# Packing ahead of the v loads, an early load of u, and a new order among the first transposes

## The chip, the cores and the metric
The kernel runs on one core of one Trainium2 chip. The metric is the device time of one execution in microseconds. The time before is the median of three runs.

## What is computed
The input is x, 16 images of 64 x 64 positions with 128 channels. One layer follows the other; the last two add their result to their input.

```python
x = x + _L0_conv_ref(_gn(x), ...)      # group norm, then a two-dimensional LSTM over rows and columns
t = _to_tokens(x)                      # (16, 4096, 128)
t = t + _L1_attn_ref(_ln_t(t), ...)    # Nystrom attention, 8 heads, 64 landmarks, + convolution of v
t = t + _L1_ffn_ref(_ln_t(t), ...)     # recurrence over the 4096 tokens
...
# in _L1_attn_ref
out = attn1 @ attn2_inv @ (attn3 @ v)
res = conv(v, conv_w)                  # 33 taps along the tokens
out = (out + res) @ w_out + b_out
return x + out
# in _L1_ffn_ref
Wx = einsum('bti,hi->bth', x, W)
Wx = (Wx - mean) * rsqrt(var + eps) * gamma + beta     # mean and var over all 65536 tokens
y = sigmoid(Wx[:, t] + y @ V.T)        # 4096 steps in turn
```

## The kernel before
Six stages follow each other: group norm, LSTM, landmarks, the inverse of attn2, output, recurrence. The change touches the last two. Engines run programs of their own and meet at semaphores. All DMAs named here are issued by SP in program order, and an SP that waits issues nothing.

**The output stage** (`output_phase`) works through 16 images `b` of 8 chunks `c` of 512 tokens, 128 slots in all. Every engine has a function `slot(b, c, ...)` with a fixed order written out by hand, and `nth(b, c)` is the running number of the chunk from 1. For a chunk:
- TensorE makes the scores (L2175), ScalarE exponentiates (`p1`, L2318), TensorE weighs with the inner matrix and a column of ones (L2185), which gives values and denominators in one. ScalarE copies them to `even` and `odd` (L2310, L2312, semaphore `denc`).
- `pack(b, c)` (L1987): SP copies the denominators of `even` and `odd` with two small DMAs to `den_packed`, 128 x 32. VectorE takes reciprocals into `rec_packed` (L2386, semaphore `rec`).
- `spread(b, c)` (L1996): SP stores `rec_packed` to the scratch row `recips` in HBM, two small DMAs. It waits for `rec` of that chunk, and at L1994 for the previous broadcast to have landed, since that one reads `recips`.
- `broadcast(b, c)` (L2003): SP loads `recips` back, each head's row repeated over 16 partitions, into `rden` (256 KB). It waits for `spread` to have landed.
- VectorE multiplies (`normalise`, L2397), adds the convolved v (L2380, `oT`), TensorE projects (L2211), VectorE adds the base and takes the moments of each token (L2366 to L2372), GpSimd scales (`norm`, L2089, tile `u`), SP stores to `scaled` (L1978), TensorE adds `u`'s products to the statistics of the recurrence (`moments`, L2224).
- In the same slot TensorE convolves a quarter of half an image's v for the next image (L2197). It needs all four pieces of that half; `load_v` (L1553) loads one piece a slot with two DMAs, 544 KB together. The last image has no v loads and no convolution.

VectorE's slot runs: maxima of chunk c + 1, `residual(c - 3)`, `merge(c - 1)`, `reciprocals(c - 1)`, `normalise(c - 2)`, `add_convolved(c - 2)`. SP's slot runs: store, base load, `spread(c - 1)`, v load, `broadcast(c - 1)`, `pack(c)`, load of the tokens. Behind the last slot come the last spread and broadcast and four stores.

**The recurrence** (`recurrence_phase`) works on blocks of 128 tokens of all images. `load_u` (L2507) loads a block of `scaled` into one of five buffers `ub`, four DMAs of 256 KB; four blocks are asked for at the start. Before the first step TensorE makes the sums of the statistics (L2630), waits for the weights (48 on `f_weights`, three DMAs issued by ScalarE's queue at L2784), transposes block 0 (`turn_first`, L2640, four groups; ScalarE copies each to `zT`, L2789), and makes the statistics' products (`spread` at L2763, and two pair products at L2766 and L2768) from which VectorE and GpSimd make scale and shift. Then come the weigh products (L2666), the normalisation, and `lay` (L2678), on which the first step stands. The fourth transposes reuse the first's bank and wait for its copy.

Of the kernel before, what the change touches and what calls it, by code (L numbers as in the profile page):

```python
# [11 lines left out]
P = 128  # L12
B = 16
G = 64
C = 128
# [16 lines left out]
class Memory:  # L32


    def __init__(self, nc, ctx):
        self.nc, self.ctx = nc, ctx
# [271 lines left out]
NG = NT // GT  # L308
# [40 lines left out]
class Kept:  # L349
# [4 lines left out]
    def __init__(self, m, sems):  # L354
        self.fwc = m.sb("k_fwc", [C, C])
        self.rstd = m.sb("k_rstd", [P, B, NT])
        self.sums = m.sb("k_sums", [P, MOMENTS])
        self.weight = m.sb("k_weight", [P, 1 + C])
        self.ready = sems.sem("k_ready")

    def fill_weight(self, pool):

# [1515 lines left out]
def output_phase(nc, sems, R, E, K, xnt, tokens, vals, recips, scaled):  # L1878


    with ExitStack() as ctx:
        m = Memory(nc, ctx)
# [43 lines left out]
        s_ust = [sems.sem(f"o_ust{k}") for k in range(2)]  # L1926
        SETUP = 4

        def nth(b, c):

            return NG * b + c + 1

        def wait(eng, name, count):

            if count > 0:
                eng.wait_ge(s[name], count)
# [27 lines left out]
        @block.sync  # L1964
        def _(sp):
            def load_tokens(b, c):
                E.load_tokens(sp, xnt, b, c)

            def load_base(b, c):
                E.load_base(sp, tokens, b, c)  # L1970

            def load_v(b, half, piece):
                E.load_v(sp, vals, b, half, piece)

            def store_scaled(b, c):
                wait(sp, "u", nth(b, c))
                b0, c0 = at(b, c)
                sp.dma_start(scaled[b0, 512 * c0:512 * c0 + 512, :].rearrange("(n p) c -> p n c", p=P), u[c % 2][:, :, 1:1 + C]  # L1978
                             ).then_inc(s_ust[c % 2], 16)

            def pack(b, c):

                wait(sp, "denc", 2 * nth(b, c))
                wait(sp, "rec", nth(b, c) - 1)
                for h, tile in enumerate((even[c % 2], odd[c % 2])):
                    row = DH * (1 - h)
                    sp.dma_start(den_packed[LM * h:LM * h + LM, :], tile[row:C:QUAD, :].rearrange("g (j e) -> g j e", j=DH)  # L1987
                                 ).then_inc(s_packed, 16)

            def spread(b, c):  # L1990

                wait(sp, "rec", nth(b, c))
                if nth(b, c) > 1:
                    sp.wait_ge(s_rden, 16 * (nth(b, c) - 1))  # L1994
                for h in range(2):
                    sp.dma_start(recips.rearrange("(g a) (j e) -> a g j e", a=2, j=DH)[h], rec_packed[LM * h:LM * h + LM, :]  # L1996
                                 ).then_inc(s_spread, 16)

            def broadcast(b, c):

                sp.wait_ge(s_spread, 32 * nth(b, c))
                wait(sp, "att", nth(b, c) - 2)
                sp.dma_start(rden[c % 2][:, :], recips.unsqueeze(1).broadcast_to([HEADS, DH, 512])).then_inc(s_rden, 16)  # L2003

            def slot(b, c, q, first, last):
                if precedes(c, 4, first):
                    store_scaled(b, c - 4)
                if precedes(c, 3, first) and follows(c, 1, last):
                    wait(sp, "res", nth(b, c - 3))
                    load_base(*at(b, c + 1))  # L2010
                if precedes(c, 1, first):
                    spread(b, c - 1)

                if c < GT and b + 1 < B:
                    wait(sp, "conv", NG * (b + 1))
                    load_v(b + 1, 1, c)
                if c >= GT and b + 2 < B:
                    wait(sp, "conv", NG * (b + 1) + GT)
                    load_v(b + 2, 0, c - GT)
                if precedes(c, 1, first):  # L2020
                    broadcast(b, c - 1)
                pack(b, c)
                if follows(c, 6, last):

                    wait(sp, "qm", nth(b, c + 2))
                    load_tokens(*at(b, c + 6))
            wait(sp, "conv", GT)
            for piece in range(GT):
                load_v(1, 0, piece)
            for c in range(4, 6):  # L2030
                wait(sp, "qm", c - 3)
                load_tokens(0, c)

            each_image(sp, slot)
            spread(B - 1, NG - 1)
            broadcast(B - 1, NG - 1)
            for c in range(NG - 4, NG):
                store_scaled(B - 1, c)
            for q in range(2):
                sp.wait_ge(s_ust[q], 16 * B * NG // 2)  # L2040
# [395 lines left out]
def recurrence_phase(nc, sems, K, scaled, ffn_v_t, gamma, beta, out):  # L2436
# [4 lines left out]
    with ExitStack() as ctx:  # L2441
        m = Memory(nc, ctx)
        UB = 5
# [15 lines left out]
        moved = m.sb("f_moved", [C, 1])  # L2459
        shift = m.sb("f_shift", [C, 1])  # L2460
        std = m.sb("f_std", [P, B, NT])
        ub = [m.sb(f"f_u{k}", [P, B, C]) for k in range(UB)]
        zT = [m.sb(f"f_zT{q}", [C, RT, B]) for q in range(2)]
        wxn = [m.sb(f"f_wxn{q}", [C, RT, B]) for q in range(2)]
        y = [m.sb(f"f_y{q}", [C, RT, B]) for q in range(2)]
# [3 lines left out]
        turned = [m.ps(f"f_turned{k}", [P, 4, C]) for k in range(2)]  # L2469
        zt = m.ps("f_zt", [C, 4, P])  # L2470
# [7 lines left out]
        s_setup = sems.sem("f_setup")  # L2478
        s_stat = sems.sem("f_stat")
        s_bn = sems.sem("f_bn")  # L2480
        s_u = [sems.sem(f"f_u{k}") for k in range(UB)]
        s_zt = sems.sem("f_zt")
        s_zc = sems.sem("f_zc")
        s_wx = sems.sem("f_wx")
# [17 lines left out]
        def _(sp):  # L2502
# [12 lines left out]
            def body(T, q, first, last):  # L2515
                for g in range(GR):
                    if not first:
                        store(T - 1, 1 - q, g)
                    if T + UB - 1 < BLOCKS:
                        load_u(T + UB - 1, g)  # L2520
            for X in range(UB - 1):
                for g in range(GR):
                    load_u(X, g)
            each_block(body)
# [99 lines left out]
        def _(pe):  # L2624
# [10 lines left out]
            def turn_first(g, bank):  # L2635

                if g == 0:
                    pe.wait_ge(s_u[0], 16 * GR)
                for j in range(4):
                    mt = nc.tensor.transpose(bank[:, j, :], ub[0][:, 4 * g + j, :], ident[:, :])  # L2640
                mt.then_inc(s_zt, 1)
# [115 lines left out]
                    if spare:  # L2757
                        keep_warm()

            for g, bank in enumerate((zt, turned[0], turned[1])):  # L2760
                turn_first(g, bank)
            pe.wait_ge(s_bn, 1)
            nc.tensor.matmul(spread, full[:, 1:1 + C], K.fwc[:, :], start=True, stop=True, skip_group_check=True).then_inc(s_stat, 1)  # L2763
            pe.wait_ge(s_zc, 1)
            turn_first(3, zt)
            nc.tensor.matmul(pair[:, 0:1], K.fwc[:, :], full[:, 0:1], start=True, stop=True, skip_group_check=True)  # L2766
            pe.wait_ge(s_bn, 2)
            nc.tensor.matmul(pair[:, 1:2], prod[:, :], one[:, :], start=True, stop=True, skip_group_check=True).then_inc(s_stat, 1)  # L2768
            for k, bank in enumerate((wxp[0], wxp[1], turned[0], turned[1])):
                at_bank = bank if k < 2 else bank[:, :, :].rearrange("c j t -> c (j t)").rearrange("c (t b) -> c t b", b=B)  # L2770
                for piece in range(PIECES):
                    weigh(0, 0, k, piece, at_bank)
# [85 lines left out]
```

## Time and profile before

| | us |
|---|---|
| median of 3 runs (5888.39 to 5891.15) | 5889.22 |
| the profiled execution | 5894.68 |
| its span, first to last instruction | 5892.9 |
| TensorE busy in the span | 5223.6 (89%) |
| VectorE busy | 3058.7 (52%) |
| ScalarE busy | 3136.4 (53%) |
| GpSimd busy | 1516.7 (26%) |
| span up to the output stage | 2514 |
| output stage | 1063 |
| recurrence | 2315 |

The profile is one execution. PE is TensorE's matmul, PEld its weight load, DVE VectorE, ACT ScalarE, POOL GpSimd, and SPq what SP issues. L with a number is a line of the kernel. Times on a row are microseconds from the start of the span. A share of busy time says little of what a stage waits for; that is read from the waits of the stage, where an engine's idle time is put down to the instruction or DMA that ended it.

### The profile page before, as it was taken

How to read it: one execution, taken by the hardware profiler on the slowest of the kernel's cores; microseconds unless marked ns; L12 is line 12 of the kernel's file. 1: busy time of each engine (PE TensorE's matmuls, PEld its weight loads, DVE VectorE, ACT ScalarE, POOL GpSimd, SP SyncE). 2: the span in 40 equal slices, each digit the busy share in tenths (PEclk: the TensorE clock that was granted, in tenths of full speed). 3: DMA queues.
4: the chain of work that ended last, by engine and by line, in shares of the span. 5: the costliest groups of instructions: out<-in, count | busy, mean ns of one | idle time of the engine just before them, and what ended most of it. 6: DMA issues, size and time to landing. Idle time of an engine off the chain costs nothing. (4 is left out here: it accounts for less than half of the span.)

```text
span 5892.9 us, 223296 instructions
## 1 busy us (share of the span) xinstructions
PE 5223.6 (89%) x97395; PEld 3271.2 (56%) x97488; DVE 3058.7 (52%) x8152; ACT 3136.4 (53%) x9108; POOL 1516.7 (26%) x1905
## 2 busy tenths in 40 slices
PE   5599999997899888799999997888888888888888
PEld 4599888896566666645555443333333333333333
DVE  8677777775888886568888882111111111111111
ACT  6455555564677776478888883333333333333333
POOL 2100000001888875246666661000000000000000
PEclk7899999999999999999999998999999999999999
DMA  9631111225887773457777762111111111111100
GB/s 389 272 116 58 58 58 58 73 77 183 253 246 236 238 243 116 103 162 207 207 208 207 204 175 66 32 32 32 34 33 32 32 33 34 32 32 32 35 18 24
DMA packets 773031, 689.32 MB, mean 117 GB/s; under 512 B 67056, under 2 KB 663024, under 8 KB 767984
## 3 DMA queue, kind: packets, MB, share of 16 engines
q1 hardware_dynamic: 754672, 575.39, 32.8%
q0 software_dynamic: 14672, 95.16, 4.0%
q8 instruction: 743, 12.17, 0.9%
q10 hardware_dynamic: 2736, 4.89, 0.2%
q14 instruction: 208, 1.70, 0.1%
HBM read 392.17 MB, written 274.89 MB: 113 GB/s over the span
## 5 line engine op out<-in xcount | busy, mean ns | idle before, releaser
L2796 ACT ACTIVATE f_y<-f_acc 128x16 f32<-128x16 f32 x4096 | 753.8, 184 | 1541.3 <-PE f_acc L2738 1541.3
L2738 PEld LDWEIGHTS f_acc<-f_y,f_vT 128*32 128x32 f32 x32768 | 644.8, 108 | 1436.7 <-ACT f_y L2796 1436.1
L2738 PE MATMUL f_acc<-f_y,f_vT 128*32 128x16 f32 x32768 | 1045.7, 193 | 278.1 <-issue 0.4
L2696 PE MATMUL f_junk<-f_idle 128*32 128x512 bf16 x8400 | 831.9, 376 | 0.0
L2578 DVE COPY f_zT<-f_zt 128x512 f32<-128x512 f32 x124 | 85.8, 692 | 1136.6 <-PE f_zt L2652 1136.6
L2355 DVE TENSOR_REDUCE o_m<-o_bank_l 128x8 bf16<-128x512 f32 x512 | 328.8, 683 | 98.7 <-PE o_bank_l L2152 98.7
L2571 DVE TENSOR_SCALAR f_wxn<-f_wxp,f_scale,f_shift 128x512 f32<-128x512 f32 x126 | 102.0, 810 | 508.8 <-PE f_wxp L2666 508.8
L1299 ACT ACTIVATE a_p<-a_s 128x512 f32<-128x512 f32 x502 | 259.2, 602 | 153.6 <-PE a_s L1166 151.7
L533 POOL DMA_DIRECT2D hidden<-l_h x46 | 34.6, 754 | 1162.8 <-DVE l_hsum L790 961.5
L712 ACT ACTIVATE l_gate<-l_pf,r_ctx 128x256 f32<-128x256 f32 (+7 forms) x512 | 202.4, 446 | 229.8 <-PE l_pf L643 229.6
L2318 ACT ACTIVATE o_p<-o_bank_s 128x512 f32<-128x512 f32 x512 | 264.4, 602 | 101.2 <-PE o_bank_s L2175 101.2
L2591 DVE SCALAR_TENSOR_TENSOR f_sum<-f_u,f_std,f_turned 128x128 f32<-128x128 f32 x512 | 143.4, 342 | 317.9 <-PE f_turned L2689 317.9
L2696 PEld LDWEIGHTS f_junk<-f_idle 128*32 128x32 bf16 x8400 | 249.9, 99 | 0.0
L1359 DVE TENSOR_REDUCE a_m3p<-a_s 128x1 f32<-128x512 f32 x360 | 223.4, 682 | 50.0 <-PE a_s L1126 48.5
L633 PE MATMUL l_pio<-l_x,r_k_lm 128*128 128x256 f32 (+7 forms) x1024 | 239.0, 356 | 0.2 <-ACT l_gate L729 0.2
L633 PE MATMUL l_pf<-l_x,r_k_lm 128*128 128x256 f32 (+7 forms) x1024 | 238.9, 356 | 0.0
L647 PE MATMUL l_pio<-l_hsum,r_ctx 128*128 128x256 f32 (+7 forms) x1024 | 238.8, 356 | 0.0
L2302 ACT ACTIVATE o_base<-o_base,r_loss,r_gain 128x128 f32<-128x128 f32 x512 | 225.4, 497 | 0.0
L2689 PE MATMUL f_turned<-f_ident,f_y 128*32 128x128 f32 x4096 | 221.3, 290 | 0.5 <-DVE f_sum L2591 0.5
L1017 POOL TENSOR_TENSOR a_r<-a_vare,a_half 128x8 f32<-128x8 f32 x128 | 209.7, 1639 | 10.0
L712 ACT ACTIVATE l_gate<-l_pio,r_ctx 128x256 f32<-128x256 f32 (+7 forms) x512 | 203.3, 450 | 14.0
L2678 PE MATMUL f_acc<-f_wxn,f_ident 128*32 128x128 f32 x4096 | 207.1, 274 | 0.8 <-issue 0.8
(323 smaller groups left out, 11466.4 us busy)
## 6 DMA issues: line engine op xcount, KB each, us to landing
o_v<-vals SPq DMA_DIRECT2D x256, 272.0 KB
a_hid<-hidden SPq DMA_DIRECT2D x112, 520.0 KB, 5.0
hidden<-l_h POOLq DMA_DIRECT2D x46, 1040.0 KB, 6.8
l_x<-skew SPq DMA_DIRECT2D x46, 1024.0 KB, 5.2
vals<-a_v SPq DMA_DIRECT2D x128, 272.0 KB, 3.6
gn_x<-in_x SPq DMA_DIRECT2D x16, 2048.0 KB, 18.0
a_xin<-in_x SPq DMA_DIRECT2D x128, 256.0 KB, 4.9
tokens<-a_t SPq DMA_DIRECT2D x128, 256.0 KB, 3.4
```

The costliest lines, as they stand in the source:

```text
L633: mm = nc.tensor.matmul(banks[c][g][:, :, rows], w[W[g]], xs, start=g in (0, 2, 3), stop=False, skip_group_check=True)
L647: mm = nc.tensor.matmul(banks[c][g][:, :, rows], w[U[g]], hsum[:, lanes[c], rows], start=False, stop=True, skip_group_check=True)
L712: nc.scalar.activation(gate[:, g, lanes[c], rows], banks[c][g][:, :, rows], ACT.Tanh if g == 2 else ACT.Sigmoid, bias=bias[BI[g]]).then_in ...
L1299: nc.scalar.activation(p3[c % 2][g][:, :], score_bank(i, c, g), ACT.Exp).then_inc(s["exp"], 1)
L1359: nc.vector.tensor_reduce(m3p[:, g, c:c + 1], bank[:, :], AX.X, ALU.max).then_inc(s["mx"], 1)
L2302: nc.scalar.activation(bs[c % 4][:, k, :], bs[c % 4][:, k, :], ACT.Identity, scale=R.gain[:, b, n:n + 1], bias=R.loss[:, b, n:n + 1]).then ...
L2318: nc.scalar.activation(p1[g][:, :], bank_s[g][:, :], ACT.Exp).then_inc(s["exp"], 1)
L2355: nc.vector.tensor_reduce(m1[:, 2 * r:2 * r + 2, LM * half:LM * half + LM].rearrange("p k (g r) -> p k g r", r=QUAD)[:, :, :, 0:2], bank_l ...
L2689: mt = nc.tensor.matmul(turned[g % 2][rows, b % 4, :], y[q][:, rows, b], ident[:, :], start=True, stop=True)
L2696: nc.tensor.matmul(junk[rows, :], idle[:, 0:QUAD], idle[:, :], start=True, stop=True)
L2738: mm = nc.tensor.matmul(acc[k % 2][rows, t, :], vT[:, rows], before, start=False, stop=True, skip_group_check=True)
L2796: nc.scalar.activation(y[q][:, step, :], acc[step // RC % 2][:, step % RC, :], ACT.Sigmoid).then_inc(s_y, 1)
```

## The change
Three things.
- In SP's slot `pack(b, c)` stands behind `spread(b, c - 1)` and ahead of the v loads and `broadcast(b, c - 1)`, instead of behind that broadcast.
- Block 0 of u gets a buffer and a semaphore that outlive the output stage (`K.head`, `K.s_head`). SP loads it behind the last broadcast and ahead of the last four stores, once the stores of chunk 2 of the last image have landed; the recurrence no longer loads it.
- Before the first step, TensorE's order is: transposes 0, product `spread`, transposes 1, the pair products, transposes 2, transposes 3. It was: transposes 0, 1, 2, `spread`, transposes 3, the pair products.

```diff
@@ class Kept
+        self.head = m.sb("k_head", [P, B, C])
+        self.s_head = sems.sem("k_head")
@@ output_phase, SP's slot
                 if precedes(c, 1, first):
                     spread(b, c - 1)
-
+                pack(b, c)
                 if c < GT and b + 1 < B:
                     wait(sp, "conv", NG * (b + 1))
                     load_v(b + 1, 1, c)
...
                 if precedes(c, 1, first):
                     broadcast(b, c - 1)
-                pack(b, c)
@@ output_phase, SP behind the slots
             spread(B - 1, NG - 1)
             broadcast(B - 1, NG - 1)
+            sp.wait_ge(s_ust[0], 8 * nth(B - 1, NG - 5))
+            for g in range(B // 4):
+                sp.dma_start(K.head[:, 4 * g:4 * g + 4, :], scaled[4 * g:4 * g + 4, 0:P, :].rearrange("b p c -> p b c")
+                             ).then_inc(K.s_head, 16)
@@ recurrence_phase
-        ub = [m.sb(f"f_u{k}", [P, B, C]) for k in range(UB)]
+        ub = [K.head] + [m.sb(f"f_u{k}", [P, B, C]) for k in range(1, UB)]
-        s_u = [sems.sem(f"f_u{k}") for k in range(UB)]
+        s_u = [K.s_head] + [sems.sem(f"f_u{k}") for k in range(1, UB)]
-            for X in range(UB - 1):
+            for X in range(1, UB - 1):
@@ recurrence_phase, TensorE before the first step
-            for g, bank in enumerate((zt, turned[0], turned[1])):
-                turn_first(g, bank)
+            turn_first(0, zt)
             pe.wait_ge(s_bn, 1)
             nc.tensor.matmul(spread, full[:, 1:1 + C], K.fwc[:, :], ...)
-            pe.wait_ge(s_zc, 1)
-            turn_first(3, zt)
+            turn_first(1, turned[0])
             nc.tensor.matmul(pair[:, 0:1], K.fwc[:, :], full[:, 0:1], ...)
             pe.wait_ge(s_bn, 2)
             nc.tensor.matmul(pair[:, 1:2], prod[:, :], one[:, :], ...).then_inc(s_stat, 1)
+            turn_first(2, turned[1])
+            pe.wait_ge(s_zc, 1)
+            turn_first(3, zt)
```

## Rows read from the trace of the kernel before

**Rows 1.** Busy time of the engines in the output stage, clock, DMA share and rate.
```profile
2514.00:3577.00 1063.00, 994.00 (x12042) 518.73 (x12040) 853.45 (x2179) 866.39 (x1794) 693.25 (x705) 0.98 0.69 193
```

**Rows 2.** Order of time, SP: first and last `spread` of 111 slots.
```profile
2579.59 0.55 SPq L1996 DMA_DIRECT2D recips<-o_rec_packed  x1
...
3469.85 1.15 SPq L1996 DMA_DIRECT2D recips<-o_rec_packed  x2
```

**Rows 3.** Waits, 2579 to 3470: who for whom: us in total, times, longest.
```profile
DVE o_rec_packed L2386 <- DMA o_den_packed<-o_odd: 56.7, 80, 1.8
...
PE o_bank_x L2211 <- DVE o_oT L2380: 23.6, 28, 2.4
...
PE o_bank_s L2197 <- DMA o_v<-vals: 6.8, 8, 1.3
```

**Rows 4.** SP's own waits in the same stretch.
```profile
SPq L1994 <- DMA o_rden<-recips: 101.5, 94, 2.1
SPq L1996 <- DVE o_rec_packed L2386: 69.6, 100, 1.8
SPq L2003 <- DMA recips<-o_rec_packed: 11.0, 22, 1.4
```

**Rows 5.** Order of time, SP, one slot: start, duration, what.
```profile
3011.47 1.14 SPq L1996 DMA_DIRECT2D recips<-o_rec_packed  x2
3012.66 1.01 SPq L1553 DMA_DIRECT2D o_v<-vals  x2
3013.85 0.63 SPq L2003 DMA_DIRECT2D o_rden<-recips  x1
3014.58 0.56 SPq L1987 DMA_DIRECT2D o_den_packed<-o_even  x1
...
3017.68 0.51 SPq L1547 DMA_DIRECT2D o_base<-tokens  x1
3019.56 1.15 SPq L1996 DMA_DIRECT2D recips<-o_rec_packed  x2
```

**Rows 6.** SP's waits between the last two of these.
```profile
SPq L1994 <- DMA o_rden<-recips: 0.6, 1, 0.6
```

**Rows 7.** Order of time, ScalarE and TensorE in that slot.
```profile
3008.56 0.59 ACT L2312 ACTIVATE o_odd<-o_bank_s 128x512 f32<-128x512 f32 x1
...
3018.12 1.11 PE L2197 MATMUL o_bank_s<-o_v,o_bands 128*64 128x256 f32 x8
```

**Rows 8.** Order of time, SP and TensorE: a late v load.
```profile
3076.80 1.01 SPq L1553 DMA_DIRECT2D o_v<-vals  x2
...
3082.82 1.11 PE L2197 MATMUL o_bank_s<-o_v,o_bands 128*64 128x256 f32 x8 [1.33 <-DMA o_v<-vals]
```

**Rows 9.** Order of time, SP: first and last `spread` of nine slots, last image.
```profile
3492.47 1.15 SPq L1996 DMA_DIRECT2D recips<-o_rec_packed  x2
...
3559.67 1.15 SPq L1996 DMA_DIRECT2D recips<-o_rec_packed  x2
```

**Rows 10.** SP's waits, 3494 to 3545, seven slots of the last image.
```profile
SPq L2003 <- DMA recips<-o_rec_packed: 10.2, 7, 2.3
SPq L1996 <- DVE o_rec_packed L2386: 6.4, 7, 1.2
```

**Rows 11.** Order of time, end of the output stage and opening of the recurrence.
```profile
3567.04 1.07 POOL L2089 TENSOR_TENSOR o_u<-o_t,k_rstd 128x512 f32<-128x512 f32 x1 [0.18 <-DMA scaled<-o_u]
...
3573.76 1.04 POOL L2089 TENSOR_TENSOR o_u<-o_t,k_rstd 128x512 f32<-128x512 f32 x1
...
3578.44 0.45 ACTq L2784 DMA_DIRECT2D f_beta<-in_L_ffn_beta  x1
...
3584.55 1.09 PE L2640 MATMUL f_zt<-f_ident,f_u 128*128 128x128 f32 x4 [5.08 <-DMA f_u<-scaled]
...
3589.28 1.95 PE L2666 MATMUL f_wxp<-f_zT,k_fwc 128*32 128x128 f32 x64 [0.35 <-ACT f_zT L2789]
```

**Rows 12.** DMA issues, 3560 to 3600: count, KB each, us to landing.
```profile
f_beta<-in_L_ffn_beta ACTq DMA_DIRECT2D x1, 0.5 KB, 3.8
```

## The prediction

> **What bounds the kernel now.** I read the busy time by stages first [rows 1]. The output stage takes 1063 us of 5892.9; the recurrence behind it, 4096 steps of TensorE and ScalarE in turn, is untouched but for its opening. So the change is decided in the output stage: 128 slots (16 images of 8 chunks), each with the same program on every engine.
>
> A slot lasts 8.02 us on the mean. Its mark here is S, the moment at which SP issues `spread`; 111 slots lie between S = 2579.59 and S = 3469.85 [rows 2]. The engines' waits in that stretch [rows 3] say what TensorE lacks: its projection (L2211) waited for VectorE's o_oT 28 times, 23.6 us, its convolution (L2197) for the v loads 8 times, 6.8 us. (23.6 + 6.8) / 111 = 0.27, so an undisturbed slot takes 7.75 us. VectorE in turn waited for the packed denominators (L2386) 80 times, 56.7 us. That row is what the change aims at; read alone it promises 0.27 us a slot.
>
> SP's own waits [rows 4] say more. Before `spread(c)` SP waits first for the previous broadcast to have landed (L1994: 94 times, 101.5 us), then for the reciprocal (L1996: 100 times, 69.6 us). The reciprocal is last, but the broadcast landed only 69.6 / 111 = 0.63 us earlier, and in 11 slots nothing but the broadcast was waited for. Two loops run through SP, one 0.6 us ahead of the other:
> - denominators: S, v loads, broadcast, pack, landing, reciprocal, next S;
> - broadcast: S, v loads, broadcast, landing, next S (the scratch row recips must be free again).
>
> One slot in full [rows 5]: S at 3011.47, v issued 3012.66, broadcast 3013.85 (S + 2.38), the first pack 3014.58, base over at 3018.19. There SP waits 0.6 us for the broadcast [rows 6], which thus landed at 3018.8, 7.3 us after S and 4.9 after its issue; 0.7 us later the reciprocal is there, and S is 3019.56. Read so, 94 slots have a landing (this one stands for them): median 7.19 us behind S and 5.99 behind v's first issue, mean 7.37 behind S; 80% lie within 5.7 to 6.8 behind v's issue.
>
> **The change part by part.**
>
> *pack(c) ahead of the v loads and the broadcast.* It is two DMA issues of 0.56 [rows 5] with gaps of 0.05, 1.21 us. Its own waits cost nothing: the o_even and o_odd that it needs were done at 3009.15 [rows 7], 3.5 us before the place (3012.66) to which it moves, and the reciprocal before it is what `spread` has just waited for. Behind it stand v and the broadcast, both 1.21 us later; tokens, store and base keep their time, since the sum of issues ahead of them is the same.
> Gained: pack's second issue goes from S + 3.7 to S + 1.8, so the reciprocal is last no more, and VectorE's 56.7 us of waiting go. Late next is the broadcast. Nothing in the rows makes its landing shorter: grouped by the time since base was issued (2 to 3.5 us before v), the medians behind v's issue are 5.9, 6.0 and 6.4 us, so the queue in front of v is as good as empty already, and v's bytes stay 1.2 us ahead of the broadcast as now.
> New slot by the median: 1.19 + 1.21 + 5.99 + 0.05 = 8.44 us. By the mean: 7.37 + 1.21 + 0.05 = 8.63, less 11.0 / 111 = 0.10 for the 22 broadcasts that waited for `spread` to land (L2003, [rows 4]) and no more would: 8.53. I take 8.45, nearest to the median, which fits most slots: +0.43, times 111 = **+48 us**. Bounds: the whole of the mean, 8.63: +68; a shift of only 0.7 us, if issues and landings that now block take up the rest: 8.05, +3. The bound below nothing is the third rival.
>
> A rule of the Trainium skill gives another result. "DMA: Bandwidth & Descriptors", section "Anatomy of one DMA — SWDGE (gpsimd) path", has about 2.0 us plus bytes / 436 GB/s for a DMA. An estimate by that page: v and broadcast (800 KB) would land 3.9 us behind v's issue, the broadcast's loop would be 6.3 us, and TensorE would bound the slot. By that rule, the trace disagrees: 5.99 us where it has 3.9.
>
> *v loads 1.2 us later.* The convolution of chunks 0 and 4 needs the half whose last piece was loaded in the slot before. In the worst case seen, v issued 3076.80, the convolution ran at 3082.82 after 1.33 us of waiting [rows 8]: landed 6.0 us behind its issue. Undisturbed, the convolution stands at S + 6.65 (3018.12, [rows 7]). With v at S + 2.4 and landings of 4.6 to 6.0 it is 0.3 to 1.7 us too late in 28 slots. In a slot of 8.45 TensorE has 0.7 us to spare, which hides most: cost 0, up to +5. Without that cover it is 28 x 0.3 to 1, 8 to 28 us.
>
> *Last image.* It has no v loads; a slot takes (3559.67 - 3492.47) / 9 = 7.47 us [rows 9]. There the broadcast is held by the landing of `spread` (L2003, 10.2 us in 7 slots, [rows 10]); pack fills just this gap and delays nothing, and the 6.4 / 7 = 0.9 us by which the reciprocal comes last go. I take 0.5 of them, as VectorE's own work is close behind: 9 x 0.5 = **-4 us** (0 to -8).
>
> *Block 0 of u in the tail.* The semaphore count it waits for is that of a store issued 20 us earlier, so it costs no wait. Four issues of 0.55 stand ahead of the last four stores, and 1 MB in front of them in the queue. Store 4 frees the buffer that L2089 takes at 3567.04 (0.18 us waited, [rows 11]); with 2.2 us of issue and the bytes in front (up to 5.4 us by the stage's mean of 193 GB/s, [rows 1], though here the stage's other loads are over) that becomes 3569 to 3574. The last product of L2089 starts at 3573.76 anyhow, behind VectorE, which covers most of this span: cost 0, up to 2.
> At the opening TensorE waited 5.08 us for u, until 3584.55 [rows 11]. Next in its way is the wait for the weights: f_beta was issued 3578.44 and takes 3.8 us to land [rows 12], 3582.2. Gain 2.3.
>
> *Statistics among the transposes.* The weigh products start at 3589.28 [rows 11], behind the fourth zT copy; the small pair products are hidden in that gap now. Afterwards the product into junk (0.63 us) and they stand ahead of the last transposes, so weigh starts 0.7 later. Scale and shift come 1.2 us earlier, which the first steps don't need, as they are laid behind the weigh products. +0.7. Opening and tail together: **-1.6 us** (-3 to +1).
>
> Sum: 48 - 4 - 1.6 = +42. The profiled execution took 5894.68 us around its span of 5892.9, 5.5 above the median of the runs, 5889.22. It becomes 5937, the median **5931 us**.
>
> **The rivals.**
> 1. *The broadcast's landing is the bound* (forecast, 0.62): slots of 8.27 to 8.6, own range 5911 to 5950.
> 2. *The shift is mostly absorbed* (0.15). SP's v issues, 1.0 us now and up to 1.9 in a fifth of the slots, no more block, and `spread`'s landing hides behind pack. Shift 0.6 to 0.8, slots of 8.0 to 8.1: 5884 to 5905. Against it: the landing doesn't depend on the gap before v.
> 3. *TensorE is the bound* (0.20), the other side. It decides once the broadcast lands within 5.3 us of v's first issue (S + 7.7). Slot 7.75, 111 x 0.27 = 30, of which late v loads take 8: -22 - 4 - 1.6, 5862; at best 5852. For it: the denominators are the wait that ends most slots now, and the skill's rule. Against it: fewer than one landing in ten is below 5.7.
> 4. *v decides on top* (0.03): landings of 6 us in all 28 slots, +28: 5960.
>
> **How the numbers follow.** The range 5856 to 5950 leaves out about 0.08 on either side. 0.2% is 12 us, about what a measurement of this kernel can tell from no change. Slower (above 5901): case 1, case 4 and a fifth of case 2, 0.68; the rest of case 2 is "same", 0.12; faster 0.20.
>
> **What would show it.** Right: the wait of L2386 for o_den_packed is gone; SP waits some 2 us at L1994 in nearly every slot and not at L1996; VectorE's L2397 waits for o_rden often, and TensorE's L2211 for o_oT behind it; S to S is 8.4, broadcast at S + 3.6. Wrong: S to S of 7.7 with little waiting at L2397 (rival 3), or L2197's wait as TensorE's longest (rival 4). The opening: the first transpose 4.7 instead of 7 us behind the stage's start.

## The result, and the profile after

The change made the kernel slower: 6003.4 us (median of 4 runs) beside 5888.8 before on the same chip, ratio 1.0197 [1.0184, 1.0209], +115 us. The profiled executions show 108 of them: spans of 6001.0 and 5892.9 us. Forecast were 5931, and a range of 5856 to 5950. The direction was right, the size was not.

All of it is in the output stage, now 1173 us long (2514 to 3686.8, where GpSimd's first instruction of the next stage starts) where it took 1064 (2514 to 3577.6) [rows 1]. TensorE's granted clock over the stage is 0.96 where it was 0.98, near its 2.4 GHz level in both; its busy time grew by 26 us, a quarter of the difference at most. DMA share and rate fell with the longer slots. The windows view of after, of the output stage and 3 us of the next; the columns are length, busy time and count of PE, PEld, DVE, ACT and POOL, then granted clock, DMA share, GB/s:

```profile
2514.00:3690.00 1176.00, 1020.28 (x12054) 532.70 (x12052) 887.16 (x2182) 869.61 (x1796) 714.93 (x710) 0.96 0.65 176
```

SP's waits after, in a stretch that holds 110 of its slots (line waited at, what ended the wait: us in total, times, longest). They answer to [rows 4]:

```profile
SPq L1996 <- DMA o_rden<-recips: 297.3, 110, 4.3
SPq L1549 <- DVE o_t L2371: 41.3, 55, 2.3
SPq L1998 <- DVE o_rec_packed L2391: 3.9, 9, 0.8
```

L1996 is the old L1994, the wait in front of `spread` for the last broadcast. It went from 94 waits of 1.1 us to 110 of 2.7: SP waits for the broadcast's landing in every slot. L1998, the old L1996, is the reciprocal's wait: from 69.6 us in 100 slots to 3.9 in 9. The denominators' loop is off the path, the broadcast's loop is all of it. The waits for `spread` to land (L2003 before) are gone.

The engines' waits in the same stretch, which answer to [rows 3]:

```profile
DVE o_att L2402 <- DMA o_rden<-recips: 133.1, 99, 2.7
ACT o_even L2315 <- PE o_bank_s L2190: 115.1, 76, 4.9
PE o_bank_x L2216 <- DVE o_oT L2385: 98.2, 75, 2.5
PE o_bank_s L2202 <- DMA o_v<-vals: 16.9, 13, 2.3
```

VectorE no longer waits for the packed denominators, it waits for the broadcast (L2402, the old L2397) in 99 slots. TensorE's projection (L2216, the old L2211) waits behind it: 98 us where it was 24.

One slot of SP's timeline after (start, us, instruction), to be laid beside [rows 5]:

```profile
3030.21 1.14 SPq L1998 DMA_DIRECT2D recips<-o_rec_packed  x2
3031.45 0.58 SPq L1989 DMA_DIRECT2D o_den_packed<-o_even  x1
3032.08 0.55 SPq L1989 DMA_DIRECT2D o_den_packed<-o_odd  x1
3032.67 1.00 SPq L1555 DMA_DIRECT2D o_v<-vals  x2
3033.78 0.62 SPq L2005 DMA_DIRECT2D o_rden<-recips  x1
3034.45 0.45 SPq L1546 DMA_DIRECT2D o_xnT<-xnt  x1
3034.94 0.97 SPq L1980 DMA_DIRECT2D scaled<-o_u  x1
3035.96 0.51 SPq L1549 DMA_DIRECT2D o_base<-tokens  x1
3039.09 1.14 SPq L1998 DMA_DIRECT2D recips<-o_rec_packed  x2
```

The broadcast is issued at S + 3.57, where it was S + 2.38. SP's list is done at 3036.5; it waits there 2.6 us for the broadcast, which lands at 3039.0, 5.3 us behind its issue. Just then VectorE's `normalise` starts, and the reciprocal had been done for 1.7 us. SP's wait in 3036.4:3039.2, and two instructions from VectorE's timeline of the same slot (in brackets the idle time before, and what ended it):

```profile
SPq L1996 <- DMA o_rden<-recips: 2.6, 1, 2.6
```

```profile
3037.04 0.34 DVE L2391 RECIPROCAL o_rec_packed<-o_den_packed 128x32 f32<-128x32 f32 x1
3039.13 0.81 DVE L2402 TENSOR_TENSOR o_att<-o_att,o_rden 128x512 f32<-128x512 f32 x1 [1.74 <-DMA o_rden<-recips]
```

Below, every kernel is read in the same way over the same 111 slots. S is the issue of `spread`, B that of the broadcast; its landing is the end of SP's wait for it, so that it is read only in slots that have such a wait. v's lead is the time from v's first issue to B. Means, worked out from SP's timelines and waits (before, 94 of the 111 slots have such a wait, after all of them):

| kernel | slot, us | B behind S | v's lead | landing behind B | landing behind v's first issue | wait for the landing, us in 111 slots | wait for the reciprocal |
|---|---|---|---|---|---|---|---|
| before | 8.02 | 2.61 | 1.41 | 4.75 | 6.16 | 101 | 68 |
| after | 8.99 | 3.63 | 1.15 | 5.27 | 6.41 | 300 | 4 |

After, the three terms make the slot: 3.63 + 5.27 + 0.10 (landing to S) = 9.00. 111 x (8.99 - 8.02) = 108 us, the whole difference of the spans; the last image gives back 2 us, and the slots outside the 111 and that image take about as much.

### The profile page after: what moved, and what is told of

Read it like the earlier page. It is cut to its first block and busy times, and to the rows that moved or that the text cites. A ratio compares the mean times of both kernels' runs of the same rounds, so it can differ in the third digit from the quotient of the medians.

```text
span 6001.0 us, 223389 instructions
## 1 busy us (share of the span) xinstructions
PE 5259.3 (88%) x97488; PEld 3287.0 (55%) x97488; DVE 3092.5 (52%) x8152; ACT 3133.1 (52%) x9108; POOL 1536.3 (26%) x1905
## 5 line engine op out<-in xcount | busy, mean ns | idle before, releaser
L2216 PE MATMUL o_bank_x<-o_wo,o_oT 128*128 128x128 f32 x1024 | 156.3, 298 | 109.6 <-DVE o_oT L2385 109.2
L2216 PEld LDWEIGHTS o_bank_x<-o_wo,o_oT 128*128 128x128 f32 x1024 | 130.7, 200 | 211.6 <-DVE o_oT L2385 210.1
L2596 DVE SCALAR_TENSOR_TENSOR f_sum<-f_u,f_std,f_turned 128x128 f32<-128x128 f32 x400 | 112.1, 343 | 202.0 <-PE f_turned L2694 202.0
```

The costliest lines, as they stand in the source:

```text
L2216: mt = nc.tensor.matmul(bank_x[:, k, :], oT[:, P * k:P * k + P], wo[:, :], start=True, stop=True)
```

## The experiments

Each edit is shown against the kernel before unless it is said otherwise. "One run" is a single execution; the four each of the kernels before and after lie within 0.15%. There the slot, a mean of 111, is the better measure. Kernels with the same order in SP's slot show how well such a mean repeats: slots of 8.99, 9.06 and 9.07 us and landings of 5.27, 5.31 and 5.26 us behind B (after, e1, e15), landings of 4.75 and 4.72 (before, e2).

### Which of the three edits it is

**e1_pack_alone**: only `pack(b, c)` is moved.

```diff
                     spread(b, c - 1)
-
+                pack(b, c)
                 if c < GT and b + 1 < B:
...
                     broadcast(b, c - 1)
-                pack(b, c)
```

> The kernel before with pack(c) moved ahead of the v loads, nothing else. If the slot order is the whole cause: 5995 to 6005, slots of 9.0 us from S to S, SP waiting for the broadcast before every spread, and the last image faster by 0.2 us a slot. If the early load of u or the new order of the transposes carries part of the loss, this kernel is 10 us or more faster than the changed one.

**e2_rest_alone**: the changed kernel with `pack` put back behind the broadcast; the early load of u and the order of the transposes stay.

```diff
                     spread(b, c - 1)
-                pack(b, c)
+
                 if c < GT and b + 1 < B:
...
                     broadcast(b, c - 1)
+                pack(b, c)
```

> The changed kernel with pack(c) put back behind the broadcast: block 0 of u in the tail and the new order among the transposes alone. By the two traces the opening is 0.6 us shorter (17.08 to 16.50 from the stage's start to the first step) and the tail 0.5 us longer (the GpSimd product waits 5.0 us for a store), so 0 within 2 us. The prediction had -1.6. The rival, that it costs, would show 5 us or more.

Measured: e1 6012.1 beside 5895.9, ratio 1.0196 [1.0179, 1.0213], slot 9.06; e2 5895.3, ratio 0.9999 [0.9990, 1.0009], slot 8.02. The moved `pack` is the whole loss. The other two edits together can't be told from nothing.

### Whether the broadcast's place sets the slot

**e3_v_pack_bc**: `pack` goes ahead of the broadcast, but v stays in front of it. B is as late as after, v as early as before.

```diff
                     load_v(b + 2, 0, c - GT)
+                pack(b, c)
                 if precedes(c, 1, first):
                     broadcast(b, c - 1)
-                pack(b, c)
```

> Order in SP's slot: spread, v loads, pack, broadcast. The broadcast is issued as late as in the changed kernel (S + 3.6), v as early as before (S + 1.2). Theory A, the broadcast lands some 6 us behind the first v issue, because v's bytes are ahead of it, and at the earliest 3.7 us behind its own issue: landing at S + 7.2 to 7.4, TensorE bounds with slots of 7.75, 5855 to 5870. Theory B, it lands 4.7 to 5.3 us behind its own issue whatever is ahead: S + 8.3 to 8.9, slots of 8.4 to 9.0, 5935 to 6000.

Measured: 5907.8, ratio 1.0022 [1.0012, 1.0031], slot 8.12, between the two expectations. B is even later than after (S + 3.80), but it lands 4.20 us behind its issue, not 5.27. One slot of SP's timeline, and its waits in 2579:3470:

```profile
3022.08 1.15 SPq L1996 DMA_DIRECT2D recips<-o_rec_packed  x2
3023.27 1.01 SPq L1553 DMA_DIRECT2D o_v<-vals  x2
3024.38 0.58 SPq L1987 DMA_DIRECT2D o_den_packed<-o_even  x1
3025.01 0.56 SPq L1987 DMA_DIRECT2D o_den_packed<-o_odd  x1
3025.66 0.60 SPq L2003 DMA_DIRECT2D o_rden<-recips  x1
```

```profile
SPq L1994 <- DMA o_rden<-recips: 191.2, 109, 2.6
SPq L1996 <- DVE o_rec_packed L2385: 7.4, 12, 1.8
```

So 1.2 us of delay for B alone cost 0.1 us a slot, while 1.2 us for v and B together cost 0.97. The reciprocal's wait is gone here as well, and the landing stands in its place. B in itself is not what counts: v is issued ahead of the broadcast, and when it is issued on time its transfer is under way while SP issues `pack`. The median landing is 6.0 us behind v's first issue before, 6.4 after and 6.7 here, where v's lead is 2.6 us; the mean behind B is 4.75, 5.27 and 4.20. So a landing goes neither by v's issue nor by B alone.

**e4_v_first**: v ahead of `spread`, so that no bytes of v follow it. The order is v, spread, pack, broadcast.

```diff
-                if precedes(c, 1, first):
-                    spread(b, c - 1)
-
                 if c < GT and b + 1 < B:
...
                 if precedes(c, 1, first):
-                    broadcast(b, c - 1)
+                    spread(b, c - 1)
                 pack(b, c)
+                if precedes(c, 1, first):
+                    broadcast(b, c - 1)
```

> Order: v loads, spread, pack, broadcast. v goes out while SP would wait for the reciprocal; the broadcast is issued at S + 2.5 with v's bytes long ahead. Theory A: it lands 3.7 to 4.2 us behind its issue, S + 6.2 to 6.7, TensorE bounds: slots of 7.7, 5850 to 5865. Theory B: S + 7.2 to 7.8, slots of 7.8 to 7.9, 5865 to 5880.

Measured: 6012.6, ratio 1.0197 [1.0180, 1.0214], slot 9.09: a miss, since neither expectation had `spread` itself held up. The broadcast lands 4.13 us behind B now, but B stands at S + 4.83. SP's waits in 2579:3470, and a slot of its timeline:

```profile
SPq L2003 <- DMA recips<-o_rec_packed: 177.2, 98, 2.7
SPq L1994 <- DMA o_rden<-recips: 47.2, 85, 1.2
```

```profile
3029.83 2.05 SPq L1996 DMA_DIRECT2D recips<-o_rec_packed  x2
3031.99 0.57 SPq L1987 DMA_DIRECT2D o_den_packed<-o_even  x1
3032.59 0.55 SPq L1987 DMA_DIRECT2D o_den_packed<-o_odd  x1
3034.86 0.60 SPq L2003 DMA_DIRECT2D o_rden<-recips  x1
```

Between 3033.1 and 3034.9 SP waits for `spread` to have landed. The two small stores of 8 KB each now have v's 544 KB in front of them, and are in `recips` only 4.8 us behind the first's issue in the mean, 5.0 in this slot. In the last image of the kernel before, which has no v, it was 2.4 us at the least and 2.7 in the mean (B at S + 2.39 and S + 2.68). v's bytes were moved from the front of one DMA to that of another on the same loop.

**e7_bc_v_332**: v behind the broadcast, its eight pieces dealt out as 3, 3, 2 and 0 to four slots. The order is spread, pack, broadcast, v.

```diff
                     spread(b, c - 1)
-
+                pack(b, c)
+                if precedes(c, 1, first):
+                    broadcast(b, c - 1)
+                lot = ((0, 3), (3, 6), (6, 8), (8, 8))[c % GT]
                 if c < GT and b + 1 < B:
                     wait(sp, "conv", NG * (b + 1))
-                    load_v(b + 1, 1, c)
+                    for n in range(*lot):
+                        load_part(b + 1, 1, n)
...
-                if precedes(c, 1, first):
-                    broadcast(b, c - 1)
-                pack(b, c)
```

> Order: spread, pack, broadcast, v loads, and v's eight DMAs of a half spread as 3, 3, 2, 0 over its four slots, so that none is due in the slot behind it. Theory A (a DMA waits for the bytes in front of it): neither spread nor broadcast has v in front; broadcast issued at S + 2.5, landed at S + 6.7, TensorE bounds: slots of 7.7 to 7.8, 30 us less than before in the first 15 images, 4 us less in the last: 0.994 of the time before. Theory B (what delays the broadcast is the number of issues and bytes of the slot, wherever they stand): slots of 8.0 or more, no gain.

Measured: 5989.5 beside 5896.8, ratio 1.0154 [1.0140, 1.0168], slot 8.85: a miss. The broadcast lands 4.22 us behind B, as it should, but v is still on its way when the next `spread` is issued. B is at S + 4.32. SP's waits and one of ScalarE's, in 2579:3470:

```profile
SPq L2009 <- DMA recips<-o_rec_packed: 163.1, 90, 3.3
SPq L2000 <- DMA o_rden<-recips: 68.3, 58, 2.4
```

```profile
ACT o_base L2310 <- DMA o_base<-tokens: 96.7, 64, 4.1
```

L2009 is the wait for `spread` to land, as in e4. The base load, queued behind v as well, comes late for ScalarE.

The changed kernel, e3, e4 and e7 together say what is special about v's old place. `spread` lands 2.4 us behind S at the soonest, and B can't come before. v is issued right behind `spread`, so its 1.0 us of issue and the first part of its transfer fall into this wait. In the other three places its bytes were in front of something on the loop that was needed at once.

**e10_half_v**: the changed order, v loaded for 64 of the 128 partitions only.

```diff
             def load_v(b, half, piece):
-                E.load_v(sp, vals, b, half, piece)
+                for side in range(2):
+                    row = 2048 * half + 512 * piece + LM * side
+                    sp.dma_start(v[half][side][0:LM, GT * piece:GT * piece + GT, :],
+                                 vals[b, row:row + 512, :].rearrange("(n p) c -> p n c", p=P)[0:LM]).then_inc(s_v[half], 16)
```

> The order spread, pack, v, broadcast, and each v load takes 64 of 128 partitions (half of v is left out). Theory A: v's bytes cost the broadcast 1.1 us (5.3 against 4.2 in the last image), so half of them cost some 0.5: landing 4.6 to 4.8 behind its issue, slots of 8.4. If v's bytes are of no account, the landing stays at 5.3.

Measured: one run of 5972.8; slot 8.64, landing 4.65 us behind B, which is at S + 3.92. The landing follows v's bytes: 4.1 to 4.2 us with none just in front (e4, e7, and the last image of after), 4.65 with half, 5.27 with all. Not all of the step to 4.65 is bytes: v's two issues took longer here, and its lead was 1.43 us, not 1.15. Behind v's first issue the landing went from 6.41 to 6.07.

### Why the landing takes 0.5 us longer than before

The landing went from 4.75 to 5.27 us behind B, and that half of the loss was in no case of the forecast. Three things changed around the broadcast. `pack`'s DMAs stand in front of v now. The tokens, the store and the base load follow the broadcast 0.69 us behind B rather than 1.95. And v's lead shrank: its median went from 1.20 to 1.10 us, its mean from 1.41 to 1.15. In the old order SP waited for `spread` between v and the broadcast in 22 slots (11.0 us, [rows 4]), and v's two issues took 1.11 us in the mean; in the new one that wait is gone and they take 1.00. The first two have experiments of their own, the third is read from the same traces below.

**e9_pack_wide**: the changed order, and `pack` copies 64 rows of the weights `wo` instead of the scattered denominators. Two DMAs of the same size in another shape.

```diff
-                    row = DH * (1 - h)
-                    sp.dma_start(den_packed[LM * h:LM * h + LM, :], tile[row:C:QUAD, :].rearrange("g (j e) -> g j e", j=DH)
+                    sp.dma_start(den_packed[LM * h:LM * h + LM, :], wo[0:LM, 0:512 // DH]
```

> The order spread, pack, v, broadcast, and pack copies 64 rows of 128 bytes of a weight instead of 4 partitions' 16 pieces each: same bytes, same issues, same waits, but spread over the partitions. The real denominators are left out. In the changed kernel the broadcast lands 5.3 us behind its issue (4.75 before). If pack's narrow source in front of v and broadcast makes the 0.5, it falls to 4.7 to 4.9 and the slot from 9.0 to 8.5; if it is what follows the broadcast, both stay.

Measured: one run of 6018.7; slot 9.13, landing 5.24. The gather from scattered partitions is not the cause. That two small DMAs stand in front of v at all was not varied by this.

**e8_small_followers**: the changed order; tokens and base are loaded for 16 of 128 partitions. **e14_small_followers_before**: the same in the order before.

```diff
-                E.load_tokens(sp, xnt, b, c)
+                sp.dma_start(xnT[c % 4][0:16, :], xnt[b, 0:16, 512 * c:512 * c + 512]).then_inc(s_xl[c % 4], 16)
...
-                E.load_base(sp, tokens, b, c)
+                sp.dma_start(bs[c % 4][0:16, :, :], tokens[b, 512 * c:512 * c + 512, :].rearrange("(n p) c -> p n c", p=P)[0:16]
+                             ).then_inc(s_bl[c % 4], 16)
```

> The order spread, pack, v, broadcast, and the loads of tokens and base behind it take 16 of 128 partitions (the rest of both is left out). If the traffic that now follows the broadcast by 0.65 us instead of 1.9 makes the 0.5 us, the broadcast lands 4.7 or less behind its issue, slots of 8.5; if it is pack in front, it stays at 5.2 to 5.3 and slots at 8.9 to 9.0.

> The kernel before, with the loads of tokens and base cut to 16 of 128 partitions (the rest is left out). If these loads' bytes hold up v and broadcast, the broadcast lands 4.2 to 4.5 behind its issue instead of 4.75 and the slot falls from 8.02 to 7.8. If only followers closer than 1 us matter, both stay.

Measured: e8 one run of 5953.8, slot 8.53, landing 4.79; e14 one run of 5877.5, slot 7.87, landing 4.50. Without most of those bytes the broadcast lands 0.48 us sooner in the new order and 0.25 in the old, so that 0.23 of the 0.52 are theirs. But 0.29 stay (4.50 to 4.79). The base load also stands ahead of `spread` and so in front of v, where it was cut as well; v's loads landed a median 3.3 us behind their issue in e8 and 3.4 in after, so that this can't be much. e11 and e16 move what follows and cut nothing.

**e11_pack_last**: the old order of v and broadcast, `pack` behind the tokens. The followers come 0.68 us behind B, as after, with nothing moved ahead of v.

```diff
                     broadcast(b, c - 1)
-                pack(b, c)
...
                     load_tokens(*at(b, c + 6))
+                pack(b, c)
```

> The kernel before, pack(c) behind the tokens' load: order spread, v, broadcast, tokens, pack. Nothing new is ahead of the broadcast; only its follower comes at 0.65 us instead of 1.9. If followers hold the broadcast up, it lands later behind its issue than before: 5.0 to 5.3 instead of 4.75. If not, 4.75. The reciprocal comes 0.5 us later either way, so the slot is 8.5 to 8.7.

Measured: one run of 5979.2; slot 8.74, landing 5.09 us behind B. The closer followers add at most 0.34 us: v's lead is 1.24 here, 0.17 shorter than before, and behind v's first issue the landing is 6.32, 0.16 more than before. SP's waits in 2579:3520:

```profile
SPq L1994 <- DMA o_rden<-recips: 161.4, 108, 2.8
SPq L1996 <- DVE o_rec_packed L2385: 126.6, 105, 2.1
```

`pack` is later here, so the reciprocal's wait is up as well (1.2 us a slot). This run tells of the landing, not of a better place.

**e15_spaced_after**: the changed order, with a wait for `pv` of the current chunk ahead of the tokens, to put the followers back. **e16_spaced_by_next**: the same with `pv` of the next chunk.

```diff
                     broadcast(b, c - 1)
-                pack(b, c)
+                wait(sp, "pv", nth(b, c))
                 if follows(c, 6, last):
```

```diff
-                pack(b, c)
                 if follows(c, 6, last):
-
+                    wait(sp, "pv", nth(b, c) + 1)
```

> The order spread, pack, v, broadcast, and SP waits before the tokens' load until TensorE has weighed this chunk (about S + 5.5), so that tokens, store and base follow the broadcast by 1.9 us or more, as in the kernel before, with all their bytes. If the follower's distance makes the longer landing, the broadcast lands 4.75 to 4.85 behind its issue instead of 5.3, slots of 8.5: some 55 us above the time before instead of 115. If the bytes in front do it, the landing stays at 5.2 to 5.3 and the slot at 9.0 or more.

> As the spaced kernel before it, whose wait had long passed when SP came to it (6 waits, 2.3 us in all), now with the weighing of the next chunk, which ends about S + 5.5. Tokens, store and base follow the broadcast by 1.9 us, with all their bytes. If the follower's distance makes the longer landing, it is 4.75 to 4.85 behind the broadcast's issue instead of 5.3 and slots are 8.5. If it stays at 5.2 to 5.3, what is in front does it, or the order as such, and slots are 9.0 or more.

Measured: e15 6020.0 beside 5897.1, ratio 1.0211 [1.0194, 1.0228], slot 9.07. Its wait was over when SP came to it nearly every time (6 waits, 2.3 us in all), the followers stayed at 0.7 us behind B, and it says nothing. In e16 they stand 1.93 us behind B, as before: 5995.6 beside 5897.1, ratio 1.0158 [1.0140, 1.0177], slot 8.81, landing 5.06. SP's waits in 2579:3470:

```profile
SPq L1994 <- DMA o_rden<-recips: 155.9, 88, 4.0
SPq L1544 <- PE o_bank_s L2184: 118.3, 97, 3.4
```

So with v and B late and the followers where they were, 0.25 us of landing (5.31 in e1 to 5.06) and 0.25 of the slot come back. The expectation had all of the 0.5 or nothing. e8 with e14 and e16 put the followers' part at 0.23 and 0.25 us, e11 at 0.34 with a shorter lead of v in it.

The rest behind B is 0.2 to 0.3 us, about what v's lead lost in the mean. Counted from v's first issue it is nearly gone:

| followers | old order | new order |
|---|---|---|
| 1.9 us behind B | 6.16 (before) | 6.21 (e16) |
| 0.7 us behind B | 6.32 (e11) | 6.41 (after) |
| tokens and base cut to an eighth | 5.92 (e14) | 5.94 (e8) |

This doesn't prove the lead to be the cause. Within the kernel before, the 56 slots with a lead under 1.3 us (mean 1.19) land 4.85 behind B and the 18 with one over 1.7 (mean 2.04) land 4.45, so that a longer lead gives back about half of its length; by that, 0.26 us less of it are worth some 0.12. And in slots with a lead under 1.3 alone (mean 1.19 in the old order, 1.11 in the new) the landing is 4.85 before and 5.03 in e16, 4.54 in e14 and 4.81 in e8: 0.2 to 0.3 us are between the two orders there as well. So v's lead is likely part of the rest, and how much is not settled; no run takes `pack`'s two DMAs from in front of v with the rest as it is. The last image, without v, grew by 0.26 (3.91 to 4.17, ten slots), but its landings before scatter from 3.5 to 5.0, so that it tells little.

### A pack that delays nothing

**e12_pack_two_buffers**: `den_packed` twice, with a semaphore each, so that `pack(b, c)` can go ahead of `spread(b, c - 1)`, into SP's idle time. **e13_two_buffers_spaced**: the same, with a wait of SP ahead of the tokens that was to put the followers back.

```diff
-        den_packed = m.sb("o_den_packed", [P, 512 // DH])
+        den_packed = [m.sb(f"o_den_packed{k}", [P, 512 // DH]) for k in range(2)]
...
-                wait(sp, "rec", nth(b, c) - 1)
+                wait(sp, "rec", nth(b, c) - 2)
...
+                pack(b, c)
                 if precedes(c, 1, first):
                     spread(b, c - 1)
-
...
                     broadcast(b, c - 1)
-                pack(b, c)
```

```diff
                     broadcast(b, c - 1)
-                pack(b, c)
+                wait(sp, "scaled", GT * (nth(b, c) - 1) + 2)
                 if follows(c, 6, last):
```

> den_packed has two buffers and pack(c) goes ahead of spread(c - 1), into the time in which SP waits anyway: order pack, spread, v, broadcast, tokens. No wait of pack's own, v and broadcast at S + 1.2 and S + 2.4 as before. The reciprocal is no more last. If the bytes and issues in front of v are the cause of the loss, the slot is bound by the broadcast's landing alone, 7.4 plus up to 0.5 for the follower at 0.65 us, or by TensorE, 7.75: slots of 7.75 to 7.95, 10 to 35 us less than before. If packing early is itself the harm, slower than before.

> As the one with two buffers, and SP waits between broadcast and tokens until ScalarE has scaled the first half of the base (about S + 3.8), so that the follower is as far behind as before. If the follower's distance counts, the broadcast lands 4.7 behind its issue and the slot is 7.75 to 7.85, 5 to 15 us less than with the follower at once. If not, equal within 3 us.

Measured: e12 5885.5, ratio 0.9993 [0.9983, 1.0003], slot 7.97; e13 5886.0, ratio 0.9998 [0.9988, 1.0007], slot 7.90. Neither can be told from the kernel before, and both are 2% faster than the changed one. e13's wait was mostly over when SP came to it (29 waits, 9.6 us in all): its followers stand 0.74 us behind B, those of e12 0.68. So e13 is e12 once more and says nothing of the followers. e12's waits of SP and of two engines in 2579:3470:

```profile
SPq L1547 <- DVE o_t L2365: 71.9, 79, 2.9
SPq L1987 <- ACT o_odd L2311: 60.5, 94, 1.5
SPq L2003 <- DMA recips<-o_rec_packed: 50.1, 61, 2.1
SPq L1994 <- DMA o_rden<-recips: 23.5, 35, 2.1
```

```profile
DVE o_att L2396 <- DMA o_rden<-recips: 38.5, 50, 2.5
PE o_bank_x L2210 <- DVE o_oT L2379: 22.6, 20, 2.4
```

The reciprocal's wait is gone and the landing is waited for in 35 slots, not 94. Yet TensorE's projection waits 22.6 us where it waited 23.6 [rows 3]. SP now waits for the denominators' copies (L1987) and for the landing of `spread`, and B slips to S + 3.0. VectorE waits for nothing packed any more, yet the slot is only 0.05 us shorter in e12 and 0.12 in e13, where [rows 3] alone promised 0.27, and no more than the measurement can tell.

## Why the prediction was right and wrong

**The bound.** Right. Read from [rows 4] it was that the broadcast's loop runs 0.6 us behind the denominators' and takes over at once. After, the landing is waited for in 110 slots, the reciprocal in 9, VectorE no more for `den_packed`, and TensorE for VectorE behind it, as the signs listed. In e12 and e13, where the denominators come early and v keeps its place, the slot stays within 0.12 us of before: of the 57 us in [rows 3] little was to be had that way.

**The shift of B.** Right: the sign named was S + 3.6, by the means 2.61 + 1.21 - 0.10 = 3.72, and it is 3.63. But v moved by more than B, from S + 1.20 to S + 2.48. "v's bytes stay 1.2 us ahead of the broadcast as now" holds for the median (1.20, now 1.10) and not for the mean (1.41, now 1.15). Rival 2's absorption took place here, between v and B, and bought nothing, as the landing didn't come sooner with B.

**The landing.** This step failed: "Nothing in the rows makes its landing shorter", and with that the sum kept 5.99 us behind v's first issue. It measured 6.41, 0.42 more. Of these 0.17 are the median taken for the mean (6.16 in the same 94 slots), and 0.25 are growth, 111 x 0.25 = 28 us. Counted from B the growth is 0.52, 111 x 0.52 = 58 us, as v's lead shrank too. I had looked for what could shorten the landing and never priced what could lengthen it. The grouping that was to show its independence looked at what stands in front of v. What stands behind the broadcast was overlooked, though the change moved it: "tokens, store and base keep their time" was said as a thing that costs nothing, and it means that they come 1.2 us closer to a broadcast that comes later. e16, and e8 with e14, show that this is worth 0.25 and 0.23 us; e11 bounds it at 0.34. Of the remainder behind B, 0.2 to 0.3 us, some 0.1 may be v's shorter lead; the cause of the rest stays open.

**Median or mean.** A small failure: the forecast took the median, "which fits most slots", 8.45 rather than 8.53. A sum over 111 slots is a matter of the mean, and this left out 9 us. The 8.53 itself took off 0.10 for the waits for `spread`, as if a sooner B had brought a sooner landing. The 0.05 from landing to S is 0.10 in the mean. By the terms of the sum: v behind S 2.48 for 2.40, the landing 6.41 for 5.99, landing to S 0.10 for 0.05, together 0.55, beside 8.99 - 8.44.

**The rule of the Trainium skill.** The estimate by "DMA: Bandwidth & Descriptors" put the landing at 3.9 us behind v's first issue. The page states its 2.0 us plus bytes / 436 GB/s for DMAs issued by GpSimd; the forecast put it to DMAs of SP. The trace disagrees again, and by more: 6.4 after. With no bytes of v just in front, the broadcast alone takes 4.1 to 4.2 us (e4, e7). It spoke for rival 3, which fell.

**v loads.** Right: TensorE's convolution waited 16.9 us in 13 slots, 6.8 in 8 before, and the slot is full with the broadcast's loop alone (9.00 of 8.99), so that this costs nothing.

**The last image.** Overrated: 7.47 to 7.23 us a slot (mean of ten), 9 x 0.24 = 2 us, not 4. The reciprocal did not stop being last there. SP's waits after in 3597:3653, beside [rows 10]:

```profile
SPq L1996 <- DMA o_rden<-recips: 8.2, 7, 1.6
SPq L1998 <- DVE o_rec_packed L2391: 4.3, 6, 1.2
```

B is at S + 2.52 there and was at 2.68: as forecast, the two `pack` issues fit into the wait for `spread` where no v fills it, and delay nothing. But the broadcast lands 4.17 us behind B, not 3.91, which takes back what the reciprocal gave.

**Tail and opening.** Right in the sum, near nothing (e2: 0.9999). GpSimd did wait in the tail, for the store queued behind block 0's 1 MB, which VectorE's work no longer covered: from the last `spread` to the next stage it is 18.38 us and was 17.90, inside the forecast's 0 to 2. From GpSimd's timeline after:

```profile
3680.59 1.04 POOL L2094 TENSOR_TENSOR o_u<-o_t,k_rstd 128x512 f32<-128x512 f32 x1 [5.02 <-DMA scaled<-o_u]
3682.95 1.04 POOL L2094 TENSOR_TENSOR o_u<-o_t,k_rstd 128x512 f32<-128x512 f32 x1
```

In the opening the first transpose stands 4.49 us behind the stage's start, forecast 4.7, and it waits for f_beta, as named. The weigh products follow 5.34 us behind it rather than 4.73: +0.6, forecast +0.7. From TensorE's timeline after:

```profile
3691.26 1.11 PE L2645 MATMUL f_zt<-f_ident,k_head 128*128 128x128 f32 x4 [2.58 <-DMA f_beta<-in_L_ffn_beta]
3696.60 1.95 PE L2671 MATMUL f_wxp<-f_zT,k_fwc 128*32 128x128 f32 x64 [0.69 <-ACT f_zT L2795]
3703.02 0.51 PE L2683 MATMUL f_acc<-f_wxn,f_ident 128*32 128x128 f32 x9 [2.07 <-issue]
```

From the stage's start to the first step it is 16.50 us and was 17.08: 0.6 shorter, where 2.3 - 0.7 = 1.6 were forecast. `lay` (L2683) paused 2.07 us in place of 0.78. "issue" means that the profile shows nothing it waited for, so that the cause stays open.

**The range.** It ended at 5950, made from one end of the landing's distribution in the old order. No case had the landing slower than before but for v in 28 slots. The bound asked for was there: 80% of the landings lay within 5.7 to 6.8 us, and 6.8 in all slots gives 1.19 + 1.21 + 6.8 + 0.05 = 9.25, some 6020. Of an input that the change touches on three sides, the row of before bounds the mean no closer than that.

## What to carry to other kernels

When a queue's engine has to wait for a small DMA to land before it can issue the next one of a chain, try the large load that nobody waits for right in that wait. It was cheapest there, since its issue and the start of its transfer fill the wait; in the three other places tried it stood in front of the chain (+0.83 to +1.07 us a slot). When DMAs are moved, price each landing from both sides: what is now in front of it and by how much, and what now follows it more closely. The wait at the head of an engine's list is worth no more than its distance to the next loop, so look at the queue's own waits before believing it.

## What the runs showed of the hardware

- A DMA's landing depends on what is issued behind it. With 544 KB just in front, 256 KB landed 5.31 us behind its own issue with the next loads and store 0.67 us behind it (e1), and 5.06 with the same ones 1.93 us behind (e16). With two of the three cut to an eighth it was 4.79 in that order (e8), and in the old one 4.50 (e14) for 4.75.
- Two stores of 8 KB landed 2.4 us at the least and 2.7 in the mean behind the first's issue with no v in front (last image of before), and 4.8 behind 544 KB of loads (e4), though they move in the other direction. The small stores found no way past the large loads.
- The same 256 KB landed in 4.1 to 4.2 us with no v just in front (e4, e7), 4.65 with 272 KB 1.43 us ahead (e10) and 5.27 with 544 KB 1.15 us ahead (after).
